# A cross-attention and feed-forward kernel: weights prepared in another step, values placed by one transfer, and three orders in place of one

## The chip, the cores and the metric

The kernel runs on one core of one Trainium2 chip. The metric is the device time of one execution in microseconds; a kernel's figure is the median of its runs. The engines are PE (TensorE, matmuls and weight loads), ACT (ScalarE), DVE (VectorE), POOL (GpSimd) and SP (SyncE, which here only issues DMAs).

## The reference

Four batches of 2048 rows of 512 numbers attend to 77 keys each, with 16 heads of 32 columns; then a feed-forward part follows, made of 64 small units with 16 inner values each.

```python
def xattn(q_src, ctx, mask, Wq, Wk, Wv, Wo):      # 16 heads, d_k = 32
    q, k, v = heads(q_src @ Wq.T), heads(ctx @ Wk.T), heads(ctx @ Wv.T)
    logits = einsum('bhqd,bhkd->bhqk', q, k) / sqrt(32)
    logits = where(mask == 0, -1e9, logits)        # mask (1, 1, 2048, 77)
    return merge(softmax(logits) @ v) @ Wo.T

def ffn(x):
    s = x @ Win + bin_                             # 512 -> 64
    h = relu(s[..., None] * W1 + b1)               # 64 units x 16
    g = einsum('btmh,mh->btm', h, W2) + b2
    return g @ Wout + bout                         # 64 -> 512

x = x + xattn(layernorm(x), ctx, mask, ...)        # x (4, 2048, 512), ctx (4, 77, 512)
x = x + ffn(layernorm(x))
```

## The kernel before

**Tiles.** The 8192 rows are cut into 16 groups of 512 rows, four groups a batch, and a group into four tiles of 128 rows (T = 4). The scores of a tile are made in two halves of eight heads, so a group has eight halves, k = 0 to 7; a half is 128 x 616 (8 x 77). Large matmuls are done as three float16 passes: each operand is split into a high part (a copy to float16 by ACT) and a low part (operand less high part, by POOL or DVE), and high x high, high x low and low x high are added up in PSUM. Names ending in `_part` are the first, `_low` the second.

**Steps.** Step i, from -2 to 17, does five parts for different groups. AHEAD, for group i+2: layernorm of x (`x_statistics`, `x_means` on DVE, `front_rstd` on POOL, `x_normal` and `x_part` on ACT, `x_low` on POOL) and the DMA transposes of its tiles into `xT` (`turn_x`, one a tile, SP). FRONT, for group i+1: q in four column blocks (`q` on PE, `q_part`, `q_low` into `qT`). SOFT, for group i: the halves 0 to 7 of scores (`logits` on PE; `maxima` on DVE, which reduces and subtracts; `exps` on ACT; `sums` on DVE; `divide` on POOL; `p_part` on ACT; `p_low` on POOL; `turn_p` on SP, which transposes a half into `pT`), then, for its first two tiles (pair 0), `pv` on PE, `a_part`, `a_low`, `wo`, `residual`, and the layernorm and transposes of h (`h_normal`, `h_part`, `h_low`, `turn_h` into `hT`). BACK, for group i-1: the same for pair 1 (its halves 4 to 7 are called -4 to -1 there), then `ffn_in` on PE, `s_part` and `s_low`, and the first four of eight chunks of inner values (`ffn_pre` on PE, which spreads s over 128 rows, and `relus` on ACT). FFN, for group i-2: chunks 4 to 7, `ffn_g`, `g_copy`, `g_low`, `ffn_out`, `output`, then `store` and, into the same slot of `xr`, `reload`. A sixth part, LATE, stands in step 0 alone: Wv and Wo are transposed on PE (L1161), v of all batches is made (L1181), and ACT and DVE copy these into `wvT`, `v_all` and `woT` (`late_values`, `late_wo`; L683, L687, L692 on ACT).

**What sets the order.** Each engine has one function `one_step`, written by hand, which lists its instructions in a fixed order for every step; parts that a step doesn't have are left out. On the compute engines steps 2 to 13 are a hardware loop of three passes of four steps, and the others are written out; SP's queue is written out whole. PSUM is shared by rings of two banks each: `tr_banks` (transposes, q, pre) and `mm_banks` (k, v, pv, wo, s, g, out). Which use takes which bank, and after which other, stands in two tables, `TR_ORDER` and `MM_ORDER`, which must match PE's order. `lg_banks` holds the scores.

**SP's queue.** It loads x, the context and the weights (L378 to L398), places the keys (`keys`, four DMAs at L405 into `k_blocks`), turns x (L429), h (L437) and p (L449), stores (L459), reloads (L376) and, between steps -1 and 0, places Wout (16 DMAs, L527, which `q_part` of step 0 waits for at L745). A head's 77 keys do not start at multiples of 128 rows of `pT`, so v is cut into 12 pieces (`CUTS`), and `values` places them with 12 DMAs (L413) from `v_all` into one of the two buffers of `v_now`. A buffer serves two groups of a batch, and `next_values` changes one in every even step: 24 DMAs in step 0 for both, 12 each in steps 2, 4, ..., 12, after `turn_p` of half 3 and ahead of the turns of x and h. The changed buffer is used two steps on.

**Staging.** Wk and Wq are loaded into the space of `pT`, Wv into a buffer of its own (`wv_raw`), Wo into `hT`, and the small weights of the feed-forward part (`spare`) into the second half of `qT`, which is why `q_part` of step 0 waits until Wout has been placed.

## Time and profile before

| what | value |
|---|---|
| median of three runs | 976.37 us (975.87 to 976.71) |
| the profiled execution | 980.87 us, its span 979.1 us |
| mean granted clock of PE | 0.928 |
| PE busy | 799.1 us (82%) |
| DVE busy | 660.0 us (67%) |
| ACT busy | 536.4 us (55%) |
| POOL busy | 529.1 us (54%) |
| DMA | 118.78 MB, 121 GB/s in the mean |

The profile is of one execution: the span runs from its first instruction to its last, and the execution's own time has 1.8 us more around it. A timeline's row is a run of like instructions on one engine: its start in us from the span's start, its length, the engine, the line of the kernel, the operation, what it writes and reads, how many there are, and in brackets how long the engine stood idle before it and what ended that. "issue" stands for idle time that no wait in the records explains. The granted clock is TensorE's, as a share of 2.4 GHz.

### The profile page before, as it was taken

What the parts mean: (1) busy time and instruction counts of PE and PEld (TensorE: products, weight loads), DVE (VectorE), ACT (ScalarE), POOL (GpSimd) and SP (SyncE); (2) the same over time, 40 slices, a digit from 0 to 9 for tenths busy, and PEclk for the clock granted to TensorE, in tenths of its full rate; (3) what the DMA queues carried; (4) which work ended last, traced back from release to release, by engine and by line L of the source; (5) the groups of instructions that cost most, each with busy time, mean ns of one, the idle gap of its engine ahead of it and who ended that gap; (6) DMA issues with size and microseconds to landing.
All of it is one profiled execution on the core that took longest, in us unless ns stands there. A gap on an engine that the chain in (4) does not pass through costs nothing.

```text
span 979.1 us, 17043 instructions
## 1 busy us (share of the span) xinstructions
PE 799.1 (82%) x5778; PEld 382.9 (39%) x5778; DVE 660.0 (67%) x1199; ACT 536.4 (55%) x835; POOL 529.1 (54%) x499
## 2 busy tenths in 40 slices
PE   6257769897989799797989796988989798987745
PEld 5123334444444445252534343443535353533221
DVE  2145257876787778686878777676888687776632
ACT  2344245746666566657484757456665748363712
POOL 5124028664757565656575665556575657455520
PEclk9678979998999999899999999898999899998988
DMA  9513026483847567564858394655666585626231
GB/s 338 129 45 59 4 54 129 89 188 76 187 101 174 103 146 136 94 146 104 185 105 177 84 190 96 133 133 115 152 129 127 112 175 113 124 58 137 60 101 44
DMA packets 336084, 118.78 MB, mean 121 GB/s; under 512 B 324652, under 2 KB 325316, under 8 KB 335992
## 3 DMA queue, kind: packets, MB, share of 16 engines
q1 hardware_dynamic: 335415, 116.97, 54.7%
q8 instruction: 50, 0.82, 0.3%
q10 hardware_dynamic: 576, 0.64, 0.2%
q14 instruction: 43, 0.34, 0.1%
HBM read 22.64 MB, written 16.78 MB: 40 GB/s over the span
## 4 chain that ended last, share of the span: by engine, by line
PE 50%; DVE 10%; issue 10%; POOL 9%; SPq 8%; ACT 7%; DMA 5%; ACTq 0%; POOLq 0%; DVEq 0%
PE mm_banks L1189 12%; PE tr_banks L1189 10%; PE lg_banks L1226 5%; SPq L413 5%; PE mm_banks L1244 5%; PE mm_banks L1290 5%; POOL p_parts L609 4%; POOL probs L603 3%; PE mm_banks L1301 3%; ACT inner L781 2%; PE tr_banks L1281 2%; PE lg_banks L1223 2%; DVE probs L984 2%; DVE row_max L980 2%; PE mm_banks L1181 2%
## 5 line engine op out<-in xcount | busy, mean ns | idle before, releaser
L609 POOL TENSOR_TENSOR p_parts<-probs,p_parts 128x616 f16<-128x616 f32 x128 | 172.6, 1355 | 89.0 <-ACT p_parts L761 87.5
L1189 PE MATMUL tr_banks<-xT,wqT 128*128 128x512 f16 x768 | 179.2, 388 | 32.9 <-DMA xT<-x_parts 27.8
L603 POOL TENSOR_TENSOR probs<-probs,row_inv 128x616 f32<-128x616 f32 x128 | 154.3, 1216 | 66.9 <-DVE row_inv L1000 66.9
L1189 PE MATMUL mm_banks<-woT,aT 128*128 128x512 f16 x768 | 173.4, 383 | 10.4 <-DVE aT L1006 5.6
L1226 PE MATMUL lg_banks<-k_blocks,qT 128*128 128x308 f16 x768 | 151.0, 313 | 0.0
L753 ACT ACTIVATE probs<-probs 128x616 f32<-128x616 f32 x128 | 89.4, 710 | 72.3 <-DVE probs L984 71.7
L587 POOL TENSOR_TENSOR x_parts<-x_normed,x_parts 128x512 f16<-128x512 f32 x64 | 74.0, 1156 | 101.5 <-ACT x_parts L722 101.3
L1189 PEld LDWEIGHTS tr_banks<-xT,wqT 128*128 128x128 f16 x768 | 73.8, 99 | 135.3 <-issue 48.3
L984 DVE TENSOR_TENSOR probs<-lg_banks,row_max 128x616 f32<-128x616 f32 x128 | 102.4, 800 | 32.6 <-POOL p_parts L609 22.5
L761 ACT ACTIVATE p_parts<-probs 128x616 f16<-128x616 f32 x128 | 90.9, 710 | 49.7 <-POOL probs L603 45.6
L1189 PEld LDWEIGHTS mm_banks<-woT,aT 128*128 128x128 f16 x768 | 74.5, 98 | 103.8 <-issue 14.4
L980 DVE TENSOR_REDUCE row_max<-lg_banks 128x8 f32<-128x616 f32 x128 | 100.7, 787 | 16.8 <-PE lg_banks L1226 14.9
L781 ACT ACTIVATE inner<-tr_banks,inner_cols,w_div 128x512 f32<-128x512 f32 x128 | 94.3, 771 | 29.2 <-PE tr_banks L1281 28.9
L994 DVE TENSOR_REDUCE row_sum<-probs 128x8 f32<-128x616 f32 x128 | 98.2, 788 | 8.4 <-issue 4.8
L1281 PE MATMUL tr_banks<-s_parts,spread 128*128 128x512 f16 x128 | 49.0, 440 | 58.8 <-DVE s_parts L1039 42.4
L1226 PEld LDWEIGHTS lg_banks<-k_blocks,qT 128*128 128x128 f16 x768 | 79.5, 104 | 41.7 <-issue 3.5
L1223 PE MATMUL lg_banks<-mask_bias,ident 128*128 128x308 bf16 x256 | 81.8, 319 | 13.7 <-issue 7.6
L592 POOL TENSOR_TENSOR h_parts<-h_normed,h_parts 128x512 f16<-128x512 f32 x64 | 74.1, 1157 | 16.6 <-ACT h_parts L740 16.6
L1244 PE MATMUL mm_banks<-pT,v_now 128*32 128x256 f16 x2304 | 70.6, 278 | 12.5 <-DMA v_now<-v_all 9.4
L712 ACT ACTIVATE x_normed<-xr,shift,rstd 128x512 f32<-128x512 f32 x64 | 51.6, 806 | 50.9 <-POOL shift L572 49.5
L765 ACT ACTIVATE aT<-mm_banks 128x512 f16<-128x512 f32 x64 | 38.1, 597 | 74.2 <-PE mm_banks L1244 74.2
L578 POOL TENSOR_TENSOR rstd<-var_eps,neg_half 128x2 f32<-128x2 f32 x32 | 22.3, 696 | 102.9 <-DVE var_eps L1028 102.9
(93 smaller groups left out, 990.9 us busy)
## 6 DMA issues: line engine op xcount, KB each, us to landing
xr<-in_x SPq DMA_DIRECT2D x32, 512.0 KB, 5.7
out_x<-xr SPq DMA_DIRECT2D x32, 512.0 KB, 2.9
pT<-p_parts SPq DMA_TRANSPOSE x128, 3.6
k_blocks<-kT_all SPq DMA_DIRECT2D x32, 38.5 KB, 2.3
pT<-in_L_xattn_Wk SPq DMA_DIRECT2D x1, 1024.0 KB, 8.9
pT<-in_L_xattn_Wq SPq DMA_DIRECT2D x1, 1024.0 KB, 13.0
wv_raw<-in_L_xattn_Wv SPq DMA_DIRECT2D x1, 1024.0 KB, 15.2
hT<-in_L_xattn_Wo SPq DMA_DIRECT2D x1, 1024.0 KB, 16.5
```

What stands on the lines that cost most here:

```text
L603: pool.tensor_tensor(block_of(k), block_of(k), inv, ALU.mult).then_inc(probs_ready, 1)
L609: pool.tensor_tensor(p_parts[:, k % PS, 1, 0:2 * LW], probs[:, k % 4, :], p_parts[:, k % PS, 0, 0:2 * LW], ALU.subtract).then_inc(p_lowere ...
L753: act.activation(probs[:, k % 4, :], probs[:, k % 4, :], ACT.Exp, scale=DK ** -0.5 / W_SCALE)\
L761: act.activation(p_parts[:, k % PS, 0, 0:2 * LW], probs[:, k % 4, :], ACT.Copy).then_inc(p_high, 1)
L781: tr.read(act.activation(inner[:, j % IN_SLOTS, :], tr.bank(step, "pre", j), ACT.Relu, bias=inner_cols[:, 1, j:j + 1], scale=w1_div[:, j:j ...
L980: dve.tensor_reduce(top, logits, AX.X, ALU.max).then_inc(max_done, 1)
L984: dve.tensor_tensor(probs_of(k), logits, top.unsqueeze(3).broadcast_to([P, 2, HC, KEYS]), ALU.subtract)\
L994: dve.tensor_reduce(row_sum[:, 0, u, :], probs[:, k % 4, :].rearrange("p (h k) -> p h k", k=KEYS), AX.X, ALU.add).then_inc(sum_done, 1)
L1189: last = pe.matmul(bank, stationary(a, c), moving(b, c), start=(n == 0), stop=(n == len(passes) - 1))
L1223: pe.matmul(bank.rearrange("p (h k) -> p h k", k=KEYS), ident16[:, :], mask_bias[:, g.slot, t, :].unsqueeze(1).broadcast_to([P, HC, KEYS]) ...
L1226: last = pe.matmul(bank, qT[:, g.parity, qp, c, rows], k_blocks[:, buffer, kp, c, :], start=False, stop=(m == 2))
L1244: last = pe.matmul(bank[rows, cols], v_now[:, buffer, b, CUTS.index(cut), DK * vp:DK * (vp + 1)], pT[:, pair, b, pp, n, :], start=((vp, pp ...
```

## The change

**Where LATE stands.** It moves from step 0 to step -2, the first, in which PE has nothing else after the keys and Wq. On ACT the copies of Wv and v now stand between Wq's copies and the first `x_normal`, and those of Wo after the last `x_part` of that step. On DVE they stand after x's statistics and means. ACT's order in the fill, before (`x_normed` is `x_normal`, `x_parts` is `x_part`, `qT` is `q_part`, `aT` the transposed Wk):

```order
L671 ACTIVATE aT<-tr_banks 128x512 x4
L674 ACTIVATE kT_all<-mm_banks 128x4x77 x4
L678 ACTIVATE wqT<-tr_banks 128x512 x4
L712 ACTIVATE x_normed<-xr,shift,rstd 128x512
L722 ACTIVATE x_parts<-x_normed 128x512
L712 ACTIVATE x_normed<-xr,shift,rstd 128x512
L722 ACTIVATE x_parts<-x_normed 128x512
L712 ACTIVATE x_normed<-xr,shift,rstd 128x512 x2
L722 ACTIVATE x_parts<-x_normed 128x512 x2
L747 ACTIVATE qT<-tr_banks 128x512 x4
```

and after (the second `aT` is the transposed Wv; `h_space` with `v_all` in it takes v):

```order
L840 ACTIVATE aT<-tr_banks 128x512 x4
L845 ACTIVATE kT_all<-mm_banks 128x4x77 x4
L851 ACTIVATE wqT<-tr_banks 128x512 x4
L856 ACTIVATE aT<-tr_banks 128x512 x4
L860 ACTIVATE h_space<-mm_banks 77x2x8x32 x4
L886 ACTIVATE x_normed<-xr,shift,rstd 128x512
L896 ACTIVATE x_parts<-x_normed 128x512
L886 ACTIVATE x_normed<-xr,shift,rstd 128x512
L896 ACTIVATE x_parts<-x_normed 128x512
L886 ACTIVATE x_normed<-xr,shift,rstd 128x512 x2
L896 ACTIVATE x_parts<-x_normed 128x512 x2
L866 ACTIVATE woT<-tr_banks 128x512 x4
L921 ACTIVATE qT<-tr_banks 128x512 x2
```

Four copies of Wv and four of v came ahead of the first `x_normal`; four of Wo stand between the last `x_part` and the first `q_part`; the next `x_normal` follows two `q_part` instead of four.

**Where things lie.** Wq and Wv change places (Wq has `wq_raw`, Wv the second half of `qT`), the small weights move from `qT` to `pT`, and `v_all` shares space with `h_normed` and `h_parts`. So some waits move. `q_part` of step 0 no longer waits for Wout's placing; `turn_p` of half 4 of group 0 does. The first `h_normal` waits until all values have been copied out of `v_all`.

**Values.** `v_now` is laid out so that a buffer is one contiguous row of 1536 numbers a partition. Batch 0 is placed with 12 DMAs in step -2 (`place_values`). In step 0 `place_rest` copies that buffer to the other with one DMA, and with 12 more makes `v_blocks`, a copy for batches 1 to 3 that is padded with zeros to the layout of `v_now`. A change of batch is then one DMA of 128 x 1536 numbers (3072 bytes a partition). It stands at the end of SP's list for a step. The keys' four DMAs, which stood there, move behind the first `turn_p` of a step. SP's queue at a change of batch, step 2, before, from the last of the twelve pieces on:

```order
L413 DMA v_now<-v_all 50x2x64
L413 DMA v_now<-v_all 27x2x64
L413 DMA v_now<-v_all 77x2x64
L429 DMA_TRANSPOSE xT<-x_parts 128x8x128
L437 DMA_TRANSPOSE hT<-h_parts 128x8x128 x2
L429 DMA_TRANSPOSE xT<-x_parts 128x8x128 x3
L437 DMA_TRANSPOSE hT<-h_parts 128x8x128 x2
L405 DMA k_blocks<-kT_all 32x8x77 x4
L449 DMA_TRANSPOSE pT<-p_parts 128x10x128 x4
L459 DMA out_x<-xr 128x1024 x2
```

and after:

```order
L480 DMA_TRANSPOSE pT<-p_parts 128x10x128
L490 DMA out_x<-xr 128x1024
L480 DMA_TRANSPOSE pT<-p_parts 128x10x128 x2
L410 DMA xr<-in_x 128x1024
L465 DMA_TRANSPOSE hT<-h_space 128x8x128 x2
L457 DMA_TRANSPOSE xT<-x_parts 128x8x128 x3
L465 DMA_TRANSPOSE hT<-h_space 128x8x128
L457 DMA_TRANSPOSE xT<-x_parts 128x8x128
L465 DMA_TRANSPOSE hT<-h_space 128x8x128
L530 DMA v_now<-v_blocks 128x1536
L480 DMA_TRANSPOSE pT<-p_parts 128x10x128 x4
```

The turns of h's tiles 2 and 3 (the first L465 row, of two) come right after the loads of x, ahead of the first turn of x, and with no v_now between them and the turns of p.

**Three orders.** `one_step` becomes `fill_step` (steps -2 to 0), `loop_step` (1 to 13) and `drain_step` (14 to 17) on every engine, each with an order of its own, and the tables of the rings get three parts to match. In `loop_step` nearly every engine's order differs from `one_step`'s. PE at the end of a loop step, before (L1223 and L1226 are `logits`, L1189 is `wo`, L1273 `ffn_in`, L1281 `ffn_pre`):

```order
L1189 MATMUL mm_banks<-woT,aT 128x512 x24
L1223 MATMUL lg_banks<-mask_bias,ident 128x308
L1226 MATMUL lg_banks<-k_blocks,qT 128x308 x3
L1223 MATMUL lg_banks<-mask_bias,ident 128x308
L1226 MATMUL lg_banks<-k_blocks,qT 128x308 x3
L1273 MATMUL mm_banks<-hT,win 64x512 x12
L1281 MATMUL tr_banks<-s_parts,spread 128x512 x2
L1223 MATMUL lg_banks<-mask_bias,ident 128x308
L1226 MATMUL lg_banks<-k_blocks,qT 128x308 x3
L1223 MATMUL lg_banks<-mask_bias,ident 128x308
L1226 MATMUL lg_banks<-k_blocks,qT 128x308 x3
L1281 MATMUL tr_banks<-s_parts,spread 128x512 x2
```

and after (L1616 and L1619 `logits`, L1582 `wo`, L1666 `ffn_in`, L1674 `ffn_pre`):

```order
L1616 MATMUL lg_banks<-mask_bias,ident 128x308
L1619 MATMUL lg_banks<-k_blocks,qT 128x308 x3
L1616 MATMUL lg_banks<-mask_bias,ident 128x308
L1619 MATMUL lg_banks<-k_blocks,qT 128x308 x3
L1582 MATMUL mm_banks<-woT,aT 128x512 x24
L1666 MATMUL mm_banks<-hT,win 64x512 x12
L1616 MATMUL lg_banks<-mask_bias,ident 128x308
L1619 MATMUL lg_banks<-k_blocks,qT 128x308 x3
L1616 MATMUL lg_banks<-mask_bias,ident 128x308
L1619 MATMUL lg_banks<-k_blocks,qT 128x308 x3
L1674 MATMUL tr_banks<-s_parts,spread 128x512 x4
```

`logits` 6 moved ahead of `wo` 0 and 1, `logits` 7 to between `ffn_in` and the first `ffn_pre`, and the four `ffn_pre` stand together. On ACT `x_part` 2 and 3 and `h_normal` 0 and 1 with `h_part` 0 now stand between `s_part` and the first of `relus`; before, `x_part` stood ahead of `s_part`, and `relus` 0 ahead of `h_part` 0. On DVE `q_low` 2 and 3 stand ahead of `s_low`, where a `maxima` stood. In `drain_step` PE has `ffn_out` 0 behind `pv` of pair 1, `ffn_out` 1 ahead of `ffn_in`, and 2 and 3 between and behind the first `ffn_pre`; on DVE `sums` 2 stands ahead of the residuals of pair 0, and on POOL `divide` and `p_low` alternate.

The core of the diff:

```diff
 def parts_of(i):
...
-    return parts + (LATE,) if i == 0 else parts
+    return parts + (LATE,) if i == -2 else parts
+
+def phase_of(step):
+    if not isinstance(step.i, int) or 0 < step.i < FIRST_FULL + LOOPED:
+        return LOOP
+    return FILL if step.i < 1 else DRAIN
...
-        v_all = sb("v_all", [KEYS, B, 2, 2 * HC, 2 * DK], F16)
-        v_now = sb("v_now", [P, 2, 2, len(CUTS), 2 * DK], F16)
-        wv_raw = sb("wv_raw", [P, C, D], F32)
+        v_blocks = sb("v_blocks", [P, B - 1, len(CUTS), 4 * DK], F16)
+        v_now = sb("v_now", [P, 2, len(CUTS), 4 * DK], F16)
+        wq_raw = sb("wq_raw", [P, C, D], F32)
...
-            def values(buffer, batch):
-                for i, (n, h, key, first, size) in enumerate(CUTS):
-                    sp.dma_start(v_now[first:first + size, buffer, :, i, :], v_all[key:key + size, batch, :, h, :])\
-                        .then_inc(v_ready[buffer], 16)
...
+                if k == 4 and g.n == 0:
+                    sp.wait_ge(wout_placed, 2 * 16 * J)
+                    sp.wait_ge(ffn_const, 4)
...
+            def place_values(step):
+                sp.wait_ge(pool_const, 15)
+                mm.wait_read(sp, step, "v", 0)
+                for i, (n, h, key, first, size) in enumerate(CUTS):
+                    sp.dma_start(v_now[first:first + size, 0, i, :], v_all[key:key + size, 0, h, :])\
+                        .then_inc(v_ready[0], 16)
+
+            def place_rest(step):
...
+                sp.wait_ge(v_ready[0], 16 * len(CUTS))
+                sp.dma_start(v_now[:, 1, :, :].rearrange("p i n -> p (i n)"),
+                             v_now[:, 0, :, :].rearrange("p i n -> p (i n)")).then_inc(v_ready[1], 16)
...
+                for i, (n, h, key, first, size) in enumerate(CUTS):
+                    sp.dma_start(v_blocks[first:first + size, :, i, :], v_all[key:key + size, 1:B, h, :])\
+                        .then_inc(v_placed, 16)
+
             def next_values(step):
...
+                buffer, batch = (0, (step.i + 2) // 4) if step.i % 4 == 2 else (1, step.i // 4)
+                if step.i % 2 == 0 and 0 < batch < B:
...
                     mm.wait_ready(sp, step, "pv", 3)
...
+                    sp.dma_start(v_now[:, buffer, :, :].rearrange("p i n -> p (i n)"),
+                                 v_blocks[:, batch - 1, :, :].rearrange("p i n -> p (i n)")).then_inc(v_ready[buffer], 16)
...
+                if step.first(0) and t == 0:
+                    act.wait_ge(v_ready[0], 16 * len(CUTS))
+                    act.wait_ge(v_placed, 16 * len(CUTS))
...
-                if step.first(0) and c == 0:
-                    act.wait_ge(wout_placed, 2 * 16 * J)
-                    act.wait_ge(ffn_const, 4 + J)
```

## Rows read from the trace of the kernel before

**Rows 1.** The windows view of one loop step; busy us and (instructions) by engine

```profile
252.70:302.50 49.80, 45.10 (x353) 21.62 (x352) 40.79 (x73) 31.97 (x51) 32.09 (x31) 1.00 0.67 147
```

**Rows 2.** PE's timeline of the fill: start, us, instruction, [idle before <- releaser]

```profile
46.10 12.60 PE L1189 MATMUL tr_banks<-xT,wqT 128*128 128x512 f16 x48 [17.30 <-DMA xT<-x_parts]
...
71.88 5.28 PE L1189 MATMUL tr_banks<-xT,wqT 128*128 128x512 f16 x12 [10.46 <-DMA xT<-x_parts]
...
92.55 0.63 PE L1161 MATMUL tr_banks<-ident,wv_raw 128*128 128x128 f32 x4 [0.43 <-DVE qT L969]
...
98.33 15.52 PE L1181 MATMUL mm_banks<-aT,inner 128*77 128x512 f32 x32 [0.89 <-ACT aT L683]
...
127.42 4.03 PE L1244 MATMUL mm_banks<-pT,v_now 128*32 128x256 f16 x72 [9.41 <-DMA v_now<-v_all]
```

**Rows 3.** ACT's timeline of the fill

```profile
29.34 0.80 ACT L712 ACTIVATE x_normed<-xr,shift,rstd 128x512 f32<-128x512 f32 x1
...
60.03 0.81 ACT L712 ACTIVATE x_normed<-xr,shift,rstd 128x512 f32<-128x512 f32 x1 [0.69 <-POOL shift L572]
...
82.28 0.60 ACT L747 ACTIVATE qT<-tr_banks 128x512 f16<-128x512 f32 x1 [6.61 <-DMA wout<-qT]
```

**Rows 4.** The timeline of SP's DMA queue in the fill

```profile
70.24 10.79 SPq L527 DMA_DIRECT2D wout<-qT  x16
...
115.31 20.77 SPq L413 DMA_DIRECT2D v_now<-v_all  x24
```

**Rows 5.** The timeline of SP's DMA queue in the loop

```profile
204.50 3.10 SPq L459 DMA_DIRECT2D out_x<-xr  x2
...
219.41 10.21 SPq L413 DMA_DIRECT2D v_now<-v_all  x12
...
231.03 2.65 SPq L437 DMA_TRANSPOSE hT<-h_parts  x2
...
258.27 2.95 SPq L459 DMA_DIRECT2D out_x<-xr  x2
...
308.04 3.11 SPq L459 DMA_DIRECT2D out_x<-xr  x2
...
837.07 3.12 SPq L459 DMA_DIRECT2D out_x<-xr  x2
```

**Rows 6.** POOL's timeline in a step of a change of batch

```profile
228.33 1.16 POOL L592 TENSOR_TENSOR h_parts<-h_normed,h_parts 128x512 f16<-128x512 f32 x1 [0.21 <-ACT h_parts L740]
```

**Rows 7.** PE's timeline in the loop

```profile
235.41 2.77 PE L1273 MATMUL mm_banks<-hT,win 128*64 128x512 f16 x12 [2.80 <-DMA hT<-h_parts]
...
286.16 1.49 PE L1273 MATMUL mm_banks<-hT,win 128*64 128x512 f16 x12
290.53 0.60 PE L1281 MATMUL tr_banks<-s_parts,spread 128*128 128x512 f16 x2 [2.88 <-DVE s_parts L1039]
290.97 0.30 PE L1223 MATMUL lg_banks<-mask_bias,ident 128*128 128x308 bf16 x1
...
292.23 0.39 PE L1281 MATMUL tr_banks<-s_parts,spread 128*128 128x512 f16 x1
...
301.70 2.76 PE L1189 MATMUL tr_banks<-xT,wqT 128*128 128x512 f16 x12
...
400.15 0.43 PE L1223 MATMUL lg_banks<-mask_bias,ident 128*128 128x308 bf16 x1 [3.64 <-issue]
```

**Rows 8.** DVE's groups of the list by line; xcount | busy, mean ns | idle before

```profile
L980 DVE TENSOR_REDUCE row_max<-lg_banks 128x8 f32<-128x616 f32 x128 | 100.7, 787 | 16.8 <-PE lg_banks L1226 14.9
...
L969 DVE TENSOR_TENSOR qT<-tr_banks,qT 128x512 f16<-128x512 f32 x64 | 42.5, 663 | 32.3 <-ACT qT L747 30.0
```

**Rows 9.** The timeline of the drain, PE and POOL

```profile
895.24 7.80 PE L1189 MATMUL mm_banks<-woT,aT 128*128 128x512 f16 x24 [4.17 <-DVE aT L1006]
...
907.66 5.34 PE L1189 MATMUL mm_banks<-woT,aT 128*128 128x512 f16 x24 [0.31 <-issue]
...
929.78 2.66 POOL L609 TENSOR_TENSOR p_parts<-probs,p_parts 128x616 f16<-128x616 f32 x2
```

More of the change, by code:

```diff
@@ new lines, in loop_step @@
+                if back:
+                    h_normal(step, 2)
+                    h_part(step, 2)
+                if soft:
+                    a_part(step, 0, 1)
+                if back:
+                    h_normal(step, 3)
+                    h_part(step, 3)
+                if ahead:
+                    x_normal(step, 0)
+                    x_part(step, 0)
+                    x_normal(step, 1)
+                    x_part(step, 1)
+                    x_normal(step, 2)
+                if front:
+                    q_part(step, 3)
@@ new lines, in loop_step @@
+                if ahead:
+                    x_normal(step, 3)
+                if soft:
+                    exps(step, 6)
+                if back:
+                    s_part(step)
+                if ahead:
+                    x_part(step, 2)
+                    x_part(step, 3)
+                if soft:
+                    h_normal(step, 0)
+                    h_normal(step, 1)
+                    h_part(step, 0)
+                if back:
+                    relus(step, 0)
+                if soft:
+                    exps(step, 7)
@@ new lines, in loop_step @@
+                if soft:
+                    maxima(step, 4)
+                    maxima(step, 5)
+                if front:
+                    q_low(step, 0)
+                if back:
+                    residual(step, 2)
+                if ahead:
+                    x_statistics(step, 0)
+                if back:
+                    residual(step, 3)
+                    h_counted(step, 1)
+                if front:
+                    q_low(step, 1)
+                if back:
+                    h_means(step, 1)
```

796 lines of the change are left out of this document (596 added, 200 removed).

## The prediction

> **What bounds the kernel now.** I read the trace in this order: the busy time of one loop step, PE's timeline of the fill with ACT and the DMA queue of SP beside it, then two neighbouring steps of the loop, then the last three steps. In the fill PE stands idle 17.30 us until x of the first group has been turned [rows 2]. Later the transposes of Wv (from 92.55) and the matmuls of v (15.52 us, from 98.33) stand in the middle of step 0, and then PE waits for v_now, until 127.42 [rows 2]. So work that needs only weights and context comes when x is there, and nothing comes while x is missing.
>
> In the loop PE is the engine that ends last, with waits of its own. The stores of out_x mark the steps: 53.77 us from 204.50 to 258.27 and 49.77 to 308.04; twelve steps, 204.50 to 837.07, take 632.6 us, 52.7 each [rows 5]. The first is a change of batch: twelve small v_now DMAs hold SP's queue for 10.21 us, so the turn of h's third and fourth tile (one row of two issues, from 231.03) goes late; GpSimd had finished that tile at 229.49 [rows 5, 6], and the second issue left some 2.8 us after that. PE waited 2.80 us for hT [rows 7]. Such a block of twelve comes six times (even steps 2 to 12; the row at 219.41 stands for them). The next step has no such wait, but in both PE waits for s_parts after it: 2.88 us in the odd one [rows 7]. Twice, at the loop's back edge, PE also waits some 3.6 us or more for nothing that the profile shows [rows 7]; the change leaves that branch.
>
> **Fill, what is lost.** ACT's new order has the copies of Wv and v before the first x_normed (order of ACT above). PE can begin on Wv where it was idle, at about 29 us. Four transposes with their copies take some 3.5 us, as from 92.55 to 98.33 at most 5.8, and the v matmuls 15.52 [rows 2]: v is done at about 48 us. So x_normed starts at 48 instead of 29.34, 18.7 us later [rows 3]. From there to q it took 16.76 us for group 0 (29.34 to 46.10, while loads were still landing) and 11.85 for group 1 (60.03 to 71.88) [rows 2, 3]. I take the second, as the loads have landed by then: q of group 0 starts at 60 us, 14 later than before. Wo's transposes and copies lie beside that chain, since ACT reaches them after the last x_parts and q needs three us more; uncovered they would cost about 4.
>
> **Fill, what is gained.** x_normed of group 1 now follows the second q copy, not the fourth, which saves two q's, about 5 us, so q of group 1 starts 9 late. ACT's wait of 6.61 us for wout's placing before q_part goes, because the staging rows moved out of qT [rows 3]; that makes up 6 of the 9 for the probabilities, though the 16 wout DMAs (10.79 us of SP) still stand ahead of the first turn of them [rows 4]. Those turns then land near 101 us. The late block and the 24 v_now DMAs (20.77 us of SP) no longer stand ahead of pv: batch 0 is placed in step -2 while SP waits for x anyway, and the rest (1 + 12 DMAs, 11 us by 10.21 for twelve) after the first four turns [rows 4, 5]. These hold up the turns of x for group 2, which before stood behind 24; no loss. So the first pv goes from 127.42 to about 101: **26 us less**. From both sides: 32 if x's chain runs as short as 11 us and Wo is wholly covered, 18 if the v matmuls run at half the clock again and Wo is not covered.
>
> **Change of batch.** One DMA, at the end of the step, takes the place of the twelve in its middle. On SP it costs what one issue costs, 0.85 us (10.21/12), so turn_h goes when GpSimd is done. That makes an even step like an odd one: of the 4.0 us between 53.77 and 49.77 I count 3.2, since other odd steps were up to 51 us; six times, **19 us**. The cover is a whole step: the new values are used from the step after next or the next but one. Keys (four DMAs) move behind the first turn of p and hold up the second by under 3 us, with GpSimd's own work ahead of the use.
>
> The padded row moves 128 x 3072 B, about 390 KB, where twelve DMAs moved about half of that. A transpose of p issued behind it may land late by what such a transfer takes; I find no such pair in the trace and let it cost between 0 and 3 us of a landing, with about 10 us of slack before pv. The Trainium skill, "DMA: Bandwidth & Descriptors", section "Queues, rings and completion order", says that descriptors of one queue are consumed in ring order on each engine, and by that the transposes of the next step would stand behind the padded rows; no run here shows it, and it would cost PE nothing as long as that slack holds.
>
> **Order of the loop.** PE now runs logits 6 before wo 0, 1 and logits 7 right after ffn_in, then all four pre. Before, the gap between ffn_in and the first pre (2.88 us) came with logits 6 ahead and logits 7 behind it, where it covered a relu (290.97 to 292.23, 1.1 us of work) [rows 7]. Now 1.1 of the gap is covered. DVE reaches s_low after two q_low (2 x 0.66) instead of a maxima (two passes, the first 0.79 and the second as long), 0.3 earlier [rows 8], but ffn_in begins 1.1 earlier too, so the gap before cover is 2.88 + 1.1 - 0.3, and 2.6 stay. The wait of pre 2 and pre 3 for relu 0 and 1 gets about 1 longer, because ACT has x_part 2, 3 and h_part 0 ahead of relu 0 and exps 7 ahead of relu 1; the wait inside pre 6, 7 and g gets 0.5 shorter. In sum PE waits about 0.7 us more per step than in an odd step: twelve steps, **8 us lost**. From both sides: if the waits fall to nothing, some 3 us less per step; if ACT's new place for x_part 2, 3 waits for their transposes, some 2 more.
>
> **Drain.** Before, step 15 has 4.17 us of waiting for aT with a cold wo behind it: 7.80 us for 24 matmuls that took 5.34 a little later [rows 9]. With two logits and an output between pv and wo I take 5 of these 6.6 as saved. sums 2 now comes before the residuals, so GpSimd's row of divides starts earlier, and its last p_low, which ended at 932.4 [rows 9], comes 2 earlier; step 14 gains about 2. Outputs 2 and 3 between pre's lie under waits except about 1 us. **8 us less**; between 0 and 13.
>
> **Sum.** -26 - 19 + 8 - 8 = -45 us. The profiled execution took 980.87 us (its span 979.1, 1.8 around it): 936 for such a one. The median of the runs is 976.37, 4.5 less than that execution; against it the forecast is **931 us**.
>
> **Rivals.** A, *the orders are better than I read them*: PE's loop waits mostly close, from 52.7 to about 48.5 a step with the back edges in. Then -26 - 50 - 10, 890 us, give or take 14. For it: a step has only 45.10 us of busy PE in one 49.80 us stretch [rows 1]; against it the chain ffn_in, s, pre, relu, g, which no order shortens. B, *the loop gives the gain back*: ACT stalls on x_part 2, 3 behind late x turns, with relu and h_normal queued behind it and SP and GpSimd behind those. Two us more per step than I count: 931 + 26, 957 us, within 12. In the trace h's turn waits 2 to 3 us on the queue where it stands behind others [rows 5, 6]; against it, x's first turns now stand right behind h's. C, **slower**: the longer run of waits from ffn_in to the second g lets PE's clock fall in every step. From the first pre at 290.53 to the q at 301.70 PE has 11.2 us in the odd step [rows 7], of which I take 1.8 as waiting: 9.4 of work at the full clock. At 1.2 GHz that doubles; less 4 us that are waits anyway it costs 5.4 per step, thirteen steps, 70 us: 1001 us. It decides from 3.5 us per step on. For it: after 10.46 us of waiting, twelve q matmuls took 5.28 us [rows 2], which is the low level; after 2.80 us of waiting, twelve ffn_in matmuls 2.77, against 1.49 in the odd step [rows 7]. Against it: the odd step kept its clock through 2.88 us of waiting (granted 1.00 in 252.7 to 302.5 [rows 1]), and no single wait I count is longer. The Trainium skill, "TensorE: Matmul & The Clock Gate", section "What's actually happening", states that the throttled clock is the default and activity releases it; by that rule C would come about if waits were closely spaced, which the even step's row bears out and the odd step's does not. D, *it doesn't do what it says*: Wv and v are merely moved ahead of x, which is true in part and in the sum already (14 us lost).
>
> **How the numbers follow.** Forecast, 914 to 945: 0.62. A: 0.15. B: 0.18. C: 0.04, the only case that ends slower; 0.01 for a step in which everything cancels. The range 904 to 956 leaves out half of A and a small part of B and C, about 0.18. Anything within 0.2%, 2 us, is what a measurement of this kernel can hardly tell from no change. Faster 0.95, same 0.01, slower 0.04.
>
> **What would show it.** In the new profile: x_normed's first start at 46 to 50 us and q's at 58 to 62; the first pv at 97 to 107; no v_now wait on PE; hT no longer ends PE's waits in the middle of the loop; even and odd steps equal within 1 us, at 49.5 to 51.5 without back edges; s_parts and inner as the main waits. It is wrong if PE waits for xT in the loop, if the granted clock of the loop falls below 0.9, or if the tail from GpSimd's last p_low to the end (46.7 us now [rows 9]) grows by more than 2.

## The result, and the profile after

The changed kernel takes **939.0 us** (937.12 to 940.80), against 976.54 for the kernel before in the same comparison: ratio 0.9616 (95% interval 0.9589 to 0.9643). The forecast was 931, the range 904 to 956. The profiled execution took 940.78 us, its span 939.1.

Both traces are cut at the same instruction, the start of `ffn_in` on PE in step 1 and in step 13 (the end of the loop); twelve steps lie between. The granted clock stands ahead of the last two numbers of a windows row.

| profiled execution of | to `ffn_in` of step 1 | steps 1 to 13 | from there to the end | span |
|---|---|---|---|---|
| before | 182.24 | 632.00 | 164.86 | 979.1 |
| after | 153.45 | 625.00 | 160.65 | 939.1 |
| forecast of the differences | -26 | -19 + 8 = -11 | -8 | -45 |
| measured differences | -28.8 | -7.0 | -4.2 | -40.0 |

**Fill.** PE's timeline of after; line numbers are those of the changed kernel (L1554 transposes of Wv and Wo, L1574 v, L1582 q, L1637 pv):

```profile
26.93 3.54 PE L1554 MATMUL tr_banks<-ident,qT 128*128 128x128 f32 x16 [0.91 <-DVE wqT L1202]
31.36 13.93 PE L1574 MATMUL mm_banks<-aT,inner 128*77 128x512 f32 x32 [0.89 <-ACT aT L856]
...
54.69 1.97 PE L1554 MATMUL tr_banks<-ident,hT 128*128 128x128 f32 x8 [8.53 <-DVE woT L1213]
57.76 12.03 PE L1582 MATMUL tr_banks<-xT,wqT 128*128 128x512 f16 x48 [1.10 <-DVE woT L1213]
...
98.92 2.15 PE L1637 MATMUL mm_banks<-pT,v_now 128*32 128x256 f16 x72 [0.42 <-DMA pT<-p_parts]
```

and ACT's, where `x_normal` comes behind the copies of v and `q_part` of step 0 waits for PE alone:

```profile
45.82 0.80 ACT L886 ACTIVATE x_normed<-xr,shift,rstd 128x512 f32<-128x512 f32 x1
...
89.72 0.60 ACT L921 ACTIVATE qT<-tr_banks 128x512 f16<-128x512 f32 x1 [1.53 <-PE tr_banks L1582]
```

The idle 17.30 us ahead of q and the late block of [rows 2] are gone, and so are the waits for v_now [rows 2] and for Wout [rows 3]. A wait of 8.53 us is left, in which ACT works on x before it copies Wo.

**Loop.** PE's waits from `ffn_in` of step 1 to that of step 14, grouped by releaser (us in total, times, longest). First after, then before:

```profile
PE tr_banks L1674 <- DVE s_parts L1332: 31.3, 13, 2.7
PE tr_banks L1674 <- ACT inner L955: 30.5, 38, 1.4
PE lg_banks L1616 <- issue: 8.8, 2, 4.5
```

```profile
PE tr_banks L1281 <- DVE s_parts L1039: 34.7, 13, 2.9
PE mm_banks L1273 <- DMA hT<-h_parts: 17.1, 6, 2.9
PE tr_banks L1281 <- ACT inner L781: 11.6, 18, 0.8
PE lg_banks L1223 <- issue: 7.6, 2, 4.0
```

The six waits for hT, the first of [rows 7] among them, are gone, and the waits for the relus (`inner`) have grown from 11.6 us (and 2.3 ahead of `ffn_g`, a row left out here) to 30.5. All steps are alike now, 51.0 to 51.8 us but for the two with a back edge (55.15 and 56.25). PE at the end of a step of after (L1666 `ffn_in`, L1674 `ffn_pre`, L1616 and L1619 `logits`):

```profile
256.67 1.49 PE L1666 MATMUL mm_banks<-hT,win 128*64 128x512 f16 x12
...
258.23 0.56 PE L1619 MATMUL lg_banks<-k_blocks,qT 128*128 128x308 f16 x3
...
261.67 0.60 PE L1674 MATMUL tr_banks<-s_parts,spread 128*128 128x512 f16 x2 [2.35 <-DVE s_parts L1332]
263.29 0.61 PE L1674 MATMUL tr_banks<-s_parts,spread 128*128 128x512 f16 x1 [1.02 <-ACT inner L955]
264.75 0.61 PE L1674 MATMUL tr_banks<-s_parts,spread 128*128 128x512 f16 x1 [0.85 <-ACT inner L955]
265.15 0.47 PE L1616 MATMUL lg_banks<-mask_bias,ident 128*128 128x308 bf16 x1
265.40 0.97 PE L1619 MATMUL lg_banks<-k_blocks,qT 128*128 128x308 f16 x3
```

Behind three waits the bias matmul takes 0.47 us and the three logits matmuls 0.97; ahead of the waits three such logits took 0.56, and in [rows 7] the bias matmul took 0.30. That is the low level, 1.2 GHz. The windows view of all steps from 1 to 14, after and then before, has the granted clock at 0.93 against 0.96:

```profile
153.45:828.39 674.94, 603.75 (x4580) 285.27 (x4579) 525.25 (x946) 415.07 (x646) 417.44 (x389) 0.93 0.63 134
```

```profile
182.24:865.11 682.87, 605.10 (x4577) 288.68 (x4576) 521.28 (x940) 415.17 (x644) 415.95 (x386) 0.96 0.62 132
```

**Drain.** The last step of after on PE (L1692 and L1694 are an output):

```profile
912.60 2.77 PE L1666 MATMUL mm_banks<-hT,win 128*64 128x512 f16 x12 [9.35 <-DMA hT<-h_space]
...
917.65 0.61 PE L1674 MATMUL tr_banks<-s_parts,spread 128*128 128x512 f16 x1 [0.78 <-DVE s_parts L1332]
918.19 0.60 PE L1692 MATMUL mm_banks<-bout_parts,ones 64*128 64x512 f16 x1
918.73 1.04 PE L1694 MATMUL mm_banks<-wout,gT 128*128 128x512 f16 x2
919.56 1.06 PE L1674 MATMUL tr_banks<-s_parts,spread 128*128 128x512 f16 x2
921.06 1.28 PE L1674 MATMUL tr_banks<-s_parts,spread 128*128 128x512 f16 x2 [0.44 <-ACT inner L955]
922.27 2.18 PE L1683 MATMUL mm_banks<-inner,w_blocks 128*32 128x512 f32 x8
```

An output stands between the first `ffn_pre` and the second, at the low level. `ffn_g` (L1683) begins 9.7 us after `ffn_in`; before it was 7.5 (L1273 is `ffn_in`, L1290 `ffn_g`):

```profile
955.55 2.77 PE L1273 MATMUL mm_banks<-hT,win 128*64 128x512 f16 x12 [10.21 <-DMA hT<-h_parts]
...
963.08 2.51 PE L1290 MATMUL mm_banks<-inner,w_blocks 128*32 128x512 f32 x8
```

### The profile page after: what moved, and what is told of

Same layout as the page of the kernel before. It is cut to its first block, busy times and chain, and to the rows that moved or that the text cites. A ratio compares the mean times of both kernels' runs of the same rounds, so it can differ in the third digit from the quotient of the medians.

```text
span 939.1 us, 16984 instructions
## 1 busy us (share of the span) xinstructions
PE 796.4 (85%) x5778; PEld 377.8 (40%) x5778; DVE 664.4 (71%) x1199; ACT 535.2 (57%) x835; POOL 530.8 (57%) x500
## 4 chain that ended last, share of the span: by engine, by line
PE 72%; DVE 10%; ACT 5%; issue 5%; POOL 3%; DMA 3%; SPq 0%; ACTq 0%; POOLq 0%; DVEq 0%
PE tr_banks L1582 17%; PE mm_banks L1582 17%; PE lg_banks L1619 9%; PE mm_banks L1637 7%; PE mm_banks L1683 5%; PE mm_banks L1694 4%; PE lg_banks L1616 3%; ACT inner L955 3%; PE tr_banks L1674 3%; PE mm_banks L1692 2%; DVE qT L1262 2%; PE mm_banks L1574 1%; POOL p_parts L719 1%; DVE probs L1277 1%; DVE row_max L1273 1%
## 5 line engine op out<-in xcount | busy, mean ns | idle before, releaser
L1582 PE MATMUL tr_banks<-xT,wqT 128*128 128x512 f16 x768 | 179.7, 386 | 6.6 <-DMA xT<-x_parts 5.4
L1582 PE MATMUL mm_banks<-woT,aT 128*128 128x512 f16 x768 | 171.0, 379 | 1.3 <-DVE aT L1299 0.6
L1619 PE MATMUL lg_banks<-k_blocks,qT 128*128 128x308 f16 x768 | 152.4, 316 | 0.0
L1273 DVE TENSOR_REDUCE row_max<-lg_banks 128x8 f32<-128x616 f32 x128 | 100.8, 787 | 65.6 <-PE lg_banks L1619 65.2
L927 ACT ACTIVATE probs<-probs 128x616 f32<-128x616 f32 x128 | 90.9, 713 | 51.3 <-DVE probs L1277 50.1
L1674 PE MATMUL tr_banks<-s_parts,spread 128*128 128x512 f16 x128 | 58.7, 479 | 70.0 <-ACT inner L955 35.2
L1582 PEld LDWEIGHTS tr_banks<-xT,wqT 128*128 128x128 f16 x768 | 73.7, 99 | 107.4 <-issue 26.3
L1582 PEld LDWEIGHTS mm_banks<-woT,aT 128*128 128x128 f16 x768 | 74.9, 98 | 88.0 <-issue 2.1
L702 POOL TENSOR_TENSOR h_space<-h_space 128x512 f16<-128x512 f32 x64 | 74.0, 1158 | 53.2 <-ACT h_space L917 53.2
L1616 PE MATMUL lg_banks<-mask_bias,ident 128*128 128x308 bf16 x256 | 82.3, 321 | 21.7 <-issue 8.8
L1619 PEld LDWEIGHTS lg_banks<-k_blocks,qT 128*128 128x128 f16 x768 | 79.9, 104 | 35.5 <-issue 0.3
L1637 PE MATMUL mm_banks<-pT,v_now 128*32 128x256 f16 x2304 | 71.6, 279 | 6.2 <-DMA pT<-p_parts 6.2
L1299 DVE SCALAR_TENSOR_TENSOR aT<-mm_banks,aT 128x512 f16<-128x512 f32 x64 | 44.1, 691 | 38.6 <-ACT aT L939 38.4
```

Source lines behind the costliest of these rows:

```text
L927: act.activation(probs[:, k % 4, :], probs[:, k % 4, :], ACT.Exp, scale=DK ** -0.5 / W_SCALE)\
L1273: dve.tensor_reduce(top, logits, AX.X, ALU.max).then_inc(max_done, 1)
L1582: last = pe.matmul(bank, stationary(a, c), moving(b, c), start=(n == 0), stop=(n == len(passes) - 1))
L1616: pe.matmul(bank.rearrange("p (h k) -> p h k", k=KEYS), ident16[:, :], mask_bias[:, g.slot, t, :].unsqueeze(1).broadcast_to([P, HC, KEYS]) ...
L1619: last = pe.matmul(bank, qT[:, g.parity, qp, c, rows], k_blocks[:, buffer, kp, c, :], start=False, stop=(m == 2))
L1637: last = pe.matmul(bank[rows, cols], v_now[:, buffer, CUTS.index(cut), DK * (2 * b + vp):DK * (2 * b + vp + 1)], pT[:, pair, b, pp, n, :], ...
```

## The experiments

Each run has the kernel before beside it; ratios are against that. The table cuts the profiled execution of each as above. Theory and rival are in the expectations.

| run | median us | ratio (interval) | to step 1 | steps 1 to 13 | to the end |
|---|---|---|---|---|---|
| the change | 939.0 | 0.9616 (0.9589 to 0.9643) | 153.45 | 625.00 | 160.65 |
| e1, old loop order | 929.89 | 0.9533 (0.9501 to 0.9564) | 155.30 | 614.28 | 158.92 |
| e2, twelve pieces | 943.05 | 0.9643 (0.9606 to 0.9679) | 155.70 | 625.31 | 160.99 |
| e3, x first | 943.09 | 0.9668 (0.9636 to 0.9699) | 156.83 | 624.56 | 160.41 |
| e4, drain as loop | 952.37 | 0.9761 (0.9728 to 0.9793) | 152.68 | 623.30 | 171.12 |
| e5, no loop | 929.22 | 0.9520 (0.9487 to 0.9553) | 154.44 | 615.71 | 158.45 |
| e6, busy waits | 924.21 | 0.9465 (0.9438 to 0.9491) | 156.88 | 608.87 | 162.05 |
| e7, relus early | 919.0 | 0.9429 (0.9397 to 0.9461) | 154.20 | 602.30 | 158.00 |
| e8, x between | 931.17 | 0.9529 (0.9496 to 0.9561) | 146.21 | 624.77 | 160.62 |
| e9, before, end place | 997.76 | 1.0239 (1.0211 to 1.0268) | 179.86 | 651.37 | 163.47 |
| e10, all and busy | 897.48 | 0.9193 (0.9165 to 0.9221) | 146.09 | 590.75 | 160.76 |
| e11, old drain | 948.44 | 0.9723 (0.9695 to 0.9750) | 154.12 | 625.62 | 165.66 |
| e12, all | 896.95 | 0.9193 (0.9165 to 0.9220) | 144.71 | 594.42 | 160.77 |

The same fill took 152.68 to 156.88 us in eight executions, so a difference of 2 us in that column says nothing. The loop of the change took 623.30 to 625.62 in five (the change, e3, e4, e8, e11).

### The loop: its order, and the one transfer

**e1.** `loop_step` is the `one_step` of before on each engine; on SP:

```diff
                     turn_p(step, 3)
-                    next_values(step)
...
                     turn_h(step, 1)
                 if ffn:
                     next_keys(step)
+                if soft:
+                    next_values(step)
```

> The changed kernel, but steps 1 to 13 in the orders of the kernel before on every engine, SP too, with the one transfer of values at the end of SP's list in place of the twelve in its middle. My theory: from ffn_in to ffn_in the old order took 50.6 us in the odd steps of before and the new one takes 51.4 in every step, because s_low, relu 0 and relu 1 come later and the clock then falls; so the old order gives 0.7 us a step back, 13 steps, 9 us: 930 us, and the granted clock of the loop goes from 0.93 to 0.97 or more. A rival: the new places on SP's queue (h ahead of x) are what made the even steps short; then PE waits for hT again and the time is 945 to 955.

The theory held. The granted clock of the steps is 0.97 in the mean, and PE waits as the odd steps of before did, with no row for hT. From `ffn_in` of step 1 to that of step 14 (155.30 to 819.63 us):

```profile
PE tr_banks L1660 <- DVE s_parts L1327: 37.2, 13, 2.9
PE tr_banks L1660 <- ACT inner L950: 12.1, 16, 1.6
...
PE mm_banks L1669 <- ACT inner L950: 2.8, 5, 0.7
```

So the batch change alone takes 632.00 to 614.28 in the old order, 17.7 us, and the new order puts 10.7 of them back.

**e2.** Twelve pieces again:

```diff
-                    sp.dma_start(v_now[:, buffer, :, :].rearrange("p i n -> p (i n)"),
-                                 v_blocks[:, batch - 1, :, :].rearrange("p i n -> p (i n)")).then_inc(v_ready[buffer], 16)
+                    for i, (n, h, key, first, size) in enumerate(CUTS):
+                        sp.dma_start(v_now[first:first + size, buffer, i, :],
+                                     v_blocks[first:first + size, batch - 1, i, :]).then_inc(v_ready[buffer], 16)
...
                     reload(step, 1)
+                if soft:
+                    next_values(step)
                 if back:
                     turn_h(step, 2)
```

> The changed kernel, but each change of batch is again twelve DMAs in the middle of SP's list (behind the turns of p and the loads of x), copied from the padded buffer piece by piece; all orders stay. My theory: SP has 8 us of idle queue there and twelve DMAs take 10.2, so the turn of h goes about 2 us late, and PE waits for hT that long in six steps: 12 us slower than the changed kernel, 951. A rival: in the new order the pieces are covered, the gain came from the orders, and the time stays within 2 us of 939.

In the loop the rival held: 625.31 against 625.00. The median, 943.05, is 4 above the change, where the rival allowed 2; of the 2.9 us between the two traces 2.3 lie in the fill. SP's queue and POOL's rows of h (the second `h_low` of the pair starts at 305.38):

```profile
296.20 9.42 SPq L531 DMA_DIRECT2D v_now<-v_blocks  x12
305.66 2.62 SPq L465 DMA_TRANSPOSE hT<-h_space  x2
```

```profile
303.02 1.16 POOL L704 TENSOR_TENSOR h_space<-h_space 128x512 f16<-128x512 f32 x1 [2.40 <-ACT h_space L919]
305.38 1.16 POOL L704 TENSOR_TENSOR h_space<-h_space 128x512 f16<-128x512 f32 x1
```

The first turn goes 1.5 us late, but the pair's second tile is ready only at 306.54, so its turn is hardly held up, and PE waits for hT 0.5 us in the whole loop. With h turned ahead of x and h itself later against the pieces, they fit.

**e9.** The other half of that question, in the kernel before:

```diff
                     turn_p(step, 3)
-                    next_values(step)
+                    if step.i == 0:
+                        next_values(step)
...
                     turn_h(step, 1)
+                    if step.i != 0:
+                        next_values(step)
```

> The kernel before with one edit: in steps 2 to 12 the twelve DMAs of values stand at the end of SP's list, behind the turns of h and ahead of the keys, where the change has its one transfer; nothing else changes. My theory: the turn of h is free then (2.5 us less in an even step), but ten us of queue now stand ahead of the turns of p, which go out some 3 us behind them today, and PE waits 4 to 6 us for pT in the next step: 985 to 995. So the place at the end needs the one transfer. A rival: the turns of p have that much slack, and the place alone gives the gain: 960 to 964.

The theory held, with a median 2.8 us above its range. Each step behind such a block takes 57 us, and PE's waits (153 to 820 us) have a row that before had not:

```profile
PE mm_banks L1247 <- DMA pT<-p_parts: 27.3, 8, 4.8
```

So in the old order the end of the list is a place for one DMA and not for twelve. Either remedy takes the wait for hT away, the one transfer at the end (e1) or the new orders, with the turns of h ahead of those of x (e2); they don't add up.

**e6.** Is it the order or the clock that costs 10.7 us? The order stays, and PE gets matmuls into its waits:

```diff
+            def keep_busy(step, count):
+                place = mm.place(step, "s", 0) + 1
+                pe.wait_ge(mm.free[place % 2], mm.laps(step) + place // 2)
+                for n in range(count):
+                    pe.matmul(mm.tensor[:, place % 2, :], wqT[:, 0, 0, 0:P], woT[:, 0, 0, :], start=True, stop=True)
+
             def ffn_pre(step, j):
+                if j < 4 and phase_of(step) is LOOP and (10, 0, 4, 3)[j]:
+                    keep_busy(step, (10, 0, 4, 3)[j])
```

> The changed kernel with 17 more matmuls per loop step on PE, whose results are overwritten: 10 in the wait for s_parts ahead of pre 0, 4 and 3 in the waits ahead of pre 2 and pre 3; nothing else changes. My theory: the clock falls to its low level behind these waits (the logits after pre 2 take 0.47 and 0.97 us against 0.30 and 0.56), and PE loses about 1.3 us of work in each step by it; with PE busy it stays at the high level, and the step goes from 51.3 to 50 to 50.5 us: 925 to 930 in all. A rival: ACT's relus set the pace there, so a faster PE only waits more for inner, and the added work is in the way; 939 to 945.

The theory held: more work, less time. The same place on PE (L1674 are the added matmuls, L1682 is `ffn_pre`):

```profile
259.31 2.32 PE L1674 MATMUL mm_banks<-woT,wqT 128*128 128x512 f16 x10
261.82 0.60 PE L1682 MATMUL tr_banks<-s_parts,spread 128*128 128x512 f16 x2 [0.19 <-DVE s_parts L1332]
...
265.44 0.30 PE L1616 MATMUL lg_banks<-mask_bias,ident 128*128 128x308 bf16 x1
265.58 0.56 PE L1619 MATMUL lg_banks<-k_blocks,qT 128*128 128x308 f16 x3
```

The logits keep the high level, and steps without a back edge take 49.4 to 50.1 us at a granted clock of 1.00. In e1 the steps at 1.00 take 49.75 to 50.05 too, and those at 0.97 up to 50.9. The new order as such costs nothing: it costs because its waits let the clock fall in every step. The Trainium skill, "TensorE: Matmul & The Clock Gate", section "What's actually happening", has the throttled clock as the default that activity releases; these rows agree.

**e7.** The waits themselves made shorter:

```diff
                     h_normal(step, 1)
-                    h_part(step, 0)
                 if back:
                     relus(step, 0)
+                    relus(step, 1)
                 if soft:
+                    h_part(step, 0)
                     exps(step, 7)
                 if back:
-                    relus(step, 1)
+                    relus(step, 2)
                 if soft:
                     h_part(step, 1)
                 if back:
-                    relus(step, 2)
                     relus(step, 3)
...
                     x_means(step)
+                if front:
+                    q_low(step, 2)
...
                 if front:
-                    q_low(step, 2)
+                    q_low(step, 3)
                 if soft:
                     h_means(step, 0)
-                if front:
-                    q_low(step, 3)
```

> The changed kernel with three moves in its loop: on ACT relu 0 and 1 come right behind h_normal 1, ahead of h_part 0 and exps 7, and relu 2 ahead of h_part 1; on DVE q_low 2 goes ahead of a_low and q_low 3 ahead of h_means, so s_low comes about 0.7 us earlier. My theory: this is what the loop's order lost against before (PE waits 2.4 us for s_parts and 2.4 for inner in each step): 1.5 to 2 us a step less, 13 steps, 915 to 920. A rival: the relus are bound by pre and its banks, and h_part is missed elsewhere; 935 to 941.

The theory held. Rows at the same place:

```profile
257.03 0.60 PE L1674 MATMUL tr_banks<-s_parts,spread 128*128 128x512 f16 x2 [1.68 <-DVE s_parts L1332]
258.73 0.39 PE L1674 MATMUL tr_banks<-s_parts,spread 128*128 128x512 f16 x1 [1.09 <-ACT inner L955]
259.40 0.39 PE L1674 MATMUL tr_banks<-s_parts,spread 128*128 128x512 f16 x1 [0.28 <-ACT inner L955]
```

The waits of 2.35, 1.02 and 0.85 us are 1.68, 1.09 and 0.28, and a step takes 50.2 in the mean in place of 52.1, back edges in both. The granted clock of the twelve steps is 0.96 in place of 0.93, so a part of this gain is the clock's.

**e5.** The loop written out:

```diff
-            with eng.Fori(0, LOOPED // 4, 1) as t:
-                for v in range(FIRST_FULL, FIRST_FULL + 4):
-                    loop_step(Step(t, v))
+            for i in range(FIRST_FULL, FIRST_FULL + LOOPED):
+                loop_step(Step(0, i))
```

> The changed kernel with steps 2 to 13 written out on the compute engines too, in place of the hardware loop of three passes; the orders are the same. My theory: the two back edges cost 4.0 and 4.9 us (the steps that hold them take 55.15 and 56.25 us against some 51.2), on PE as a wait of 4 to 4.5 us for nothing that the profile shows, so written out it is 8 to 9 us faster: 930. A rival: PE waits for its instructions to be loaded, and three times as many instructions bring such waits to other places; 937 to 950.

The theory held: steps 1 to 13 take 9.3 us less, the eight steps from 309 to 719 us take 51.20 to 51.22 each, and PE has no long wait for "issue".

### The fill

**e3.** ACT's order in step -2, with SP's `place_values` behind `turn_x`:

```diff
+                    x_normal(step, 0)
+                    x_part(step, 0)
+                    x_normal(step, 1)
+                    x_part(step, 1)
+                    x_normal(step, 2)
+                    x_normal(step, 3)
+                    for c in range(C):
+                        wv_copy(step, c)
+                    v_copy(step, 0)
+                    x_part(step, 2)
+                    x_part(step, 3)
...
-                    late_values(step)
```

> The changed kernel, but in step -2 ACT does the first x_normal and x_part ahead of the copies of Wv and v, and SP places the values behind the turns of x. My theory: the first q waits for ACT's late x_normal (45.82 us), as the prediction said, and PE stands idle 8.5 us in that time; with x first it starts behind v and Wo at about 51 instead of 57.8, and the first pv comes 6 us earlier: 933. A rival: the copies of v then hold up PE instead, or the probabilities wait for Wout's placing anyway; the first pv stays at 97 to 99 and the time at 938 or 939.

The theory fell in this form. The rival's mechanism held, with the copies of Wv in the place of those of v, but it cost more than the rival said: the first pv comes at 102.67, not at 97 to 99, and the median is 943.09. ACT, and then PE:

```profile
34.67 0.81 ACT L886 ACTIVATE x_normed<-xr,shift,rstd 128x512 f32<-128x512 f32 x1 [5.21 <-POOL shift L682]
```

```profile
40.18 1.97 PE L1566 MATMUL tr_banks<-ident,qT 128*128 128x128 f32 x8 [8.51 <-ACT aT L856]
...
62.99 10.52 PE L1594 MATMUL tr_banks<-xT,wqT 128*128 128x512 f16 x48 [0.91 <-DVE woT L1225]
```

The first x_normed can't start at 29.34 as in [rows 3]: the new order of DVE has the low parts of the keys and of Wq ahead of x's statistics, so POOL's shift is late. Wv's copies then stand behind four x_normed, and PE waits 8.51 us for them.

**e8.** Wv's copies first, x between the copies of v:

```diff
+                    for c in range(C):
+                        wv_copy(step, c)
+                    x_normal(step, 0)
+                    x_part(step, 0)
+                    v_copy(step, 0)
+                    x_normal(step, 1)
+                    x_part(step, 1)
+                    v_copy(step, 1)
...
-                    late_values(step)
```

> The changed kernel, but in step -2 ACT does x_normal and x_part in the gaps between the four copies of v (2.84 us each, where it waits for PE), Wv's copies staying first, and SP places the values behind the turns of x. Theory: x first failed because Wv's copies came late and PE waited 8.5 us for them; with Wv first, v ends as in the changed kernel (45 us) and x is turned by 51, so q starts at 51 to 53 instead of 57.8, the first pv at 92 to 94, and the time is 933. A rival: the chain from q to pv is set by POOL or DVE in steps 0 and 1 and gives it back; the first ffn_in stays at 153 to 157 us and the time at 938 to 943.

The theory held:

```profile
52.21 10.52 PE L1595 MATMUL tr_banks<-xT,wqT 128*128 128x512 f16 x48 [0.91 <-DVE woT L1226]
...
91.89 2.15 PE L1650 MATMUL mm_banks<-pT,v_now 128*32 128x256 f16 x72 [0.42 <-DMA pT<-p_parts]
```

So ACT's place for x costs the change 5.5 us at q, 7.0 at the first pv and, against the mean of the eight, 8 at the first `ffn_in`. SP's half of the edit only lets the early x through: in the change the values have been issued at 45.90, ahead of x's first turn at 48.54.

### The drain

**e4.** `drain_step` is left out and the table of the drain is that of the loop:

```diff
-            run(pe, fill_step, loop_step, drain_step)
+            run(pe, fill_step, loop_step, loop_step)
```

> The changed kernel, but steps 14 to 17 run in the order of its loop. My theory: the drain's own order covers the wait for aT and lets POOL finish earlier, worth 5 to 8 us up to ffn_in of step 16, and it gives 3 back in the last step, where outputs run between the pre's at the low clock; so without it the time is 3 to 5 us longer, 942 to 944. A rival: it gives nothing, since the granted clock of the drain fell from 0.89 to 0.81; 939 or a little less.

**e11.** `drain_step` is the `one_step` of before on each engine.

> The changed kernel, but steps 14 to 17 in the orders of the kernel before on every engine. The prediction counted 8 us for the drain's new orders; the two traces show 4.2 from the ffn_in of step 13 to the end. My theory: it is these 4, since outputs between the pre's cost the clock in the last two steps: 942 to 944. A rival: the loop's slow clock and late relus hid a part of the gain, and the old orders lose the full 8 to 10, as the loop's new order did there: 947 to 950.

The loop's new order in the drain costs 10.5 us by the traces (171.12 against 160.65), more than I expected (the median is 952.37, with 942 to 944 expected), and the order of before 5.0 (165.66). By the medians e11 is 9.4 above the change; its profiled execution, 947.16, is 6.4 above that of the change, so the size stays between 5 and 9. In e11 the rival's number came, but the trace of steps 13 to the end is nearer to my theory's 4; I can't tell them apart.

### Together

**e12** has the edits of e5, e7 and e8, and **e10** those and `keep_busy` with (7, 0, 4, 1) in place of (10, 0, 4, 3).

> As the run with all four moves, but without the added matmuls: x_normal between the copies of v, relus and s_low early, the loop written out. My theory: 939 - 7 - 20 - 9 = 903, and the difference from the run with the added matmuls is what PE's clock still costs, 10 to 15 us. A rival: the relus early had already saved the clock, and both runs are within 3 us of each other.

> The changed kernel with the moves of four earlier runs together: x_normal between the copies of v in the fill, relu 0 to 2 and s_low early in the loop, the loop written out, and added matmuls in PE's waits (7 ahead of pre 0, 4 ahead of pre 2, 1 ahead of pre 3; their results are overwritten). My theory: these gains lie in different places and add up, but for the clock, of which relus early have taken a part: 939 - 7 - 20 - 9 - 10 to 15 is 888 to 893. A rival: with the waits gone another engine or the transposes of h become the bound: 900 to 905.

The gains add up: 897 us in e12, 8% below the kernel before, where I expected 903. e10 can't be told from it: its 897.48 lies above the 888 to 893 that I expected and below its rival's 900 to 905. So e12's rival held: by the medians the added matmuls bring nothing here. The windows view of three steps of e12, and then of one of e10:

```profile
194.27:243.29 49.02, 45.11 (x353) 21.58 (x352) 41.02 (x73) 31.95 (x51) 32.09 (x31) 1.00 0.71 147
243.29:292.75 49.46, 45.89 (x353) 21.97 (x352) 41.12 (x73) 32.05 (x51) 32.14 (x31) 0.97 0.62 144
292.75:342.74 49.99, 46.84 (x353) 21.94 (x353) 41.02 (x73) 32.01 (x51) 32.11 (x31) 0.93 0.64 146
```

```profile
195.72:244.75 49.03, 47.71 (x365) 22.68 (x365) 41.02 (x73) 31.95 (x51) 32.11 (x31) 1.00 0.66 147
```

With the relus early the clock often holds by itself, and a step at 1.00 takes 49.02 us with or without the added work. In these rows a step at 0.97 takes 0.4 more and one at 0.93 1.0 more; but other steps of e12 at 0.97 take 49.04 to 50.71, so the clock is not all of it. Over the twelve steps e10 is 3.7 us shorter, and the medians don't show it. What holds a step at 49.0, with PE busy for 45.1 of it, no run tested.

## Why the prediction was right, and where it was off

**Fill, right.** Forecast -26, measured -28.8 in this pair; two fills of the kernel before (182.24, and 179.86 in e9) and eight of the changed one (154.6 in the mean) give -26.4. The steps of the working held: x_normed at 45.82 (forecast 48), q at 57.76 (60), the first pv at 98.92 (101). What the working left out is DVE's new order, which makes x's shift late; it costs nothing as long as ACT comes late anyway (e3). That x is late because of Wv and v, rival D's true part, was right: x_normed comes 16.5 us later than in [rows 3]; in e8 it comes 11.3 earlier than in the change (34.56), and 8 of these reach the first `ffn_in`.

**Batch change, right in size.** Forecast -19; e1 gives -17.7, and the wait named, hT in six steps, is the one that went. The cover that was asked of the padded row held: in the six cases the turn of p right behind it lands 3.7 to 4.3 us after its issue, and the first one of the other loop steps, where none stands ahead, after 3.4 to 4.0. That is some half a us, where the prediction allowed 0 to 3, and PE waits for no pT in the loop. The latest of the six and one of the others, rows of the DMA view of 528 to 531 and of 268 to 271 us (the last number is us to landing):

```profile
pT<-p_parts SPq DMA_TRANSPOSE x1, 4.3
```

```profile
pT<-p_parts SPq DMA_TRANSPOSE x1, 3.4
```

What I didn't see is that the new orders would have removed the same wait with the twelve pieces (e2). Taken first they give -6.7 (632.00 to 625.31), and the one transfer then 0.3; so the -17.7 and the +10.7 below are the prices for one sequence of the two.

**Order of the loop, right in sign and nearly in size, wrong in part of its mechanism.** Forecast +8, measured +10.7 (e1 to after). The prediction counted longer waits, 0.7 us a step, at an unchanged clock. PE's waits for s_parts and inner did grow as counted, from 52.1 us in e1 to 61.8 over thirteen steps, 0.7 a step; but the steps of e6, with the same order, show that a step loses nothing when the clock is kept. This is the mechanism of rival C, which the prediction set aside because no single wait was longer than one through which the odd step had kept its clock. Three waits in a row, 2.35, 1.02 and 0.85 us, were enough. Its price was not 5.4 us a step but 1.3 (52.1 to 50.7 in e6), since the low level lasts only a few us of each step.

**Drain, half as large.** Forecast -8, measured -4.2. Up to `ffn_in` of step 16 the new orders gain 7.2 us (141.31 before, 134.15 after), where the prediction's terms make 9; behind it they lose 2.9, where it counted about 1. The step that failed is "Outputs 2 and 3 between pre's lie under waits except about 1 us": in step 16 `ffn_g` begins 2.1 us later after `ffn_in` than before, with an output at the low level between two pre's, and the last outputs, most of them at the low level too, make 0.7 more. In e4 and e11, whose orders have no output there, `ffn_g` begins 8.2 and 7.5 us after `ffn_in`; no run moved these outputs alone. The sign that the prediction had named came too: the tail from GpSimd's last p_low, which now ends at 887.83, is 51.3 us long against 46.7 in [rows 9]. A part of that is that this p_low ends earlier, 109.4 us after `ffn_in` of step 13 against 118.2.

```profile
886.48 1.35 POOL L719 TENSOR_TENSOR p_parts<-probs,p_parts 128x616 f16<-128x616 f32 x1 [0.89 <-ACT p_parts L935]
```

**Sum.** -45 against -40 in the profiled executions. Of the 8 us between forecast and median, these are 5; the other 3 are the profiled executions themselves, of which that of before lay 4.5 us above its median and that of after 1.8. The steps without a back edge, 51.0 to 51.8 us, lie a little above the 49.5 to 51.5 that the prediction named.

**Rivals.** B didn't come: x_part 2 and 3 wait for no turn of x in the loop. A, better orders, was no property of this change, but most of its size was there to be had: e12 has steps of 49.0 to 50.7, where A had 48.5 in the mean.

## What to carry to other kernels

Price an order by its waits and by what they do to PE's clock: here three short waits close together cost the clock too, and work that is thrown away paid where it filled them, until the waits themselves were shorter (e10). Before twelve transfers are made one, look whether their place in the queue is what delays the next one; here either remedy was enough, and the two together brought no more than one. When one engine's early work is moved ahead, give its gaps to the chain that it displaced.

## What the runs showed of the hardware that I had not expected

A back edge of the hardware loop held PE some 4 us (8.8 us in the two of after, ended by nothing that the profile shows). Written out, with every step its own instructions, the loop ran without such a wait (e5), and the two queues that bring instructions moved no more: 0.99 MB, against 1.16 in the change. And 17 matmuls more in each step, ten of which take 2.32 us and all of which are overwritten, made the kernel 15 us faster (e6), because the others then ran at 2.4 GHz (granted clock 1.00 in every step without a back edge, 0.93 in the change).
